# The second half's convolution of chunks 1 to 3 as four TensorE products in a Mamba and mixture-of-experts kernel

## The reference

```python
xn = _layernorm(x)
# s = Mamba block of xn
xr = xn * rsqrt(mean(xn * xn) + eps) * norm_w
xi, z = split(xr @ W_in)                        # 128 -> 256 and 256
xc = silu(causal_conv(xi, conv_w, 4 taps) + conv_b)
dt, Bm, Cm = split(xc @ W_x, [64, 80])          # 64, 16, 16
dt = softplus(dt @ W_dt + b_dt)                 # 256
dA = exp(dt[..., None] * A); dBu = (dt * xc)[..., None] * Bm[:, :, None, :]
h = scan(h = dA * h + dBu)                      # 256 x 16 states, over 256 tokens
y = (einsum('blds,bls->bld', h, Cm) + D_skip * xc) * silu(z)
s = xn + y @ W_out
# g = silu(mixture of experts of xn)
logits = xn @ Wg; top 2 of softmax, normalised -> scores
g = silu(sum_e scores_e * (relu(xn @ W1_e + b1_e) @ W2_e + b2_e))
out = x + s * g
```

## Time and profile before

| | |
|---|---|
| median of 3 runs | 275.86 us (275.59 to 277.68) |
| the profiled execution's own time | 278.05 us |
| its span, first to last instruction | 276.0 us |
| mean granted TensorE clock | 0.968 |
| busy: PE, DVE, ACT, POOL | 252.0, 249.0, 228.3, 237.0 us |
| instructions | 4179 |

### The profile page before, as it was taken

The page is one execution under the profiler, slowest core; times in us unless marked ns, Lnnn a source line. Parts: engine busy times, 40 slices in busy tenths (PEclk is TensorE's granted clock), DMA queues, the critical chain, the costliest instruction groups (busy, mean ns, idle before and its releaser), DMA issues. The chain is left out here.

```text
span 276.0 us, 4179 instructions
## 1 busy us (share of the span) xinstructions
PE 252.0 (91%) x1227; PEld 133.2 (48%) x1227; DVE 249.0 (90%) x284; ACT 228.3 (83%) x436; POOL 237.0 (86%) x191
## 2 busy tenths in 40 slices
PE   7889597699999899899999999789999999999992
PEld 7434241274546433445656426237647446566442
DVE  4696999949799999999999999998799999999994
ACT  1589996989979999999789899996788986878560
POOL 5509699739899999879999999977989997999995
PEclk9999999689999999999999999957999999999999
DMA  5987980024490660024670058070399700000002
GB/s 155 234 250 186 224 203 4 7 77 91 93 207 14 148 159 0 2 70 96 134 180 1 0 126 181 2 161 11 80 207 210 191 2 0 2 0 0 2 1 76
DMA packets 18979, 26.16 MB, mean 95 GB/s; under 512 B 6615, under 2 KB 12174, under 8 KB 18958
## 3 DMA queue, kind: packets, MB, share of 16 engines
q1 hardware_dynamic: 18066, 24.71, 38.1%
q10 hardware_dynamic: 700, 0.66, 1.0%
q0 software_dynamic: 192, 0.52, 0.9%
HBM read 8.65 MB, written 1.31 MB: 36 GB/s over the span
## 5 line engine op out<-in xcount | busy, mean ns | idle before, releaser
L445 POOL TENSOR_TENSOR hc<-hs,Ct 128x1024 f32<-128x1024 f32 x63 | 149.3, 2382 | 5.7 <-DMA Ct<-bc_rows 2.0
L951 DVE TENSOR_TENSOR_SCAN hs<-dec,pdbu 128x1024 f32<-128x1024 f32 x62 | 139.4, 2273 | 0.0
L638 ACT ACTIVATE dec<-rep,negA 128x512 f32<-128x512 f32 x124 | 85.0, 724 | 0.3 <-DMA rep<-dt_u 0.2
L927 DVE TENSOR_TENSOR pdbu<-rep,px 128x1024 f32<-128x1024 f32 x60 | 70.9, 1218 | 8.2 <-PE px L1174 8.1
L1200 PEld LDWEIGHTS px<-w,hT 128*128 128x128 f32 x512 | 62.5, 197 | 14.0 <-issue 8.9
L1194 PE MATMUL px<-xnT,w 128*128 128x512 f32 x128 | 64.9, 614 | 2.2 <-DVE pdbu L927 1.3
L1200 PE MATMUL px<-w,hT 128*128 128x128 f32 x512 | 65.7, 284 | 0.2 <-DVE pdbu L927 0.2
L578 POOL TENSOR_TENSOR acc<-acc,ysc 128x512 f32<-128x512 f32 x30 | 38.3, 1276 | 14.8 <-ACT ysc L752 14.8
L763 ACT ACTIVATE hT<-px,cols 128x512 f32<-128x512 f32 x64 | 43.4, 693 | 8.0 <-PE px L1194 5.5
L752 ACT ACTIVATE ysc<-px,score 128x128 f32<-128x128 f32 x120 | 34.0, 367 | 16.7 <-PE px L1200 16.6
L1083 PE MATMUL py<-hc,rsel 128*32 128x512 f32 x252 | 36.1, 619 | 1.7 <-POOL hc L445 1.7
(11 more groups left out here) (162 smaller groups left out, 275.9 us busy)
## 6 DMA issues: line engine op xcount, KB each, us to landing
rep<-dt_u SPq DMA_DIRECT2D x116, 128.0 KB, 2.4
Ct<-bc_rows SPq DMA_DIRECT2D x16, 256.0 KB, 5.2
w<-in_L_ffn_W SPq DMA_DIRECT2D x1, 1024.0 KB
...
```

Of the source, the lines that this page charges most:

```text
L445: eng.tensor_tensor(hc[:, n % HC_RING], hs[:, n % HS_RING], Ct[:, k % 2, j:j + 1, :].to_broadcast([P, 2, CH]), ALU.mult).then_inc(hc_last ...
L638: act.activation(dec[:, n % DEC_RING, i, :], rep[:, q, 0, :], ACT.Exp, scale=negA[:, q, j:j + 1])\
L927: dve.tensor_tensor(pdbu[:, at:at + 2, :], rep[:, 2 * pair:2 * pair + 2, 1, :], B[:, None, :].to_broadcast([P, 2, CH]), ALU.mult).then_inc ...
L951: dve.tensor_tensor_scan(states.rearrange("p b t -> p (b t)"), dec[:, n % DEC_RING].rearrange("p b t -> p (b t)"), pdbu[:, at:at + 2, :].r ...
```

## The change

`xc1` of chunks 1 to 3 becomes four products like `xc0`, evacuated once by ACT; the tiles `xi`, `add_tap`, the steps `taps` and ACT's wait on `convolved` go. `v0` and `v1` read all 128 rows of `dtp` with a `wdt` that is zero in its lower half (a memset on DVE), and the second copy `dt_low` goes. The selectors of `e0`, `e1` and `spread_u` have 32 rows, at partitions 0 to 31 for the first and 32 to 63 for the second, and both spreads of u follow `e1`; `B1` moves behind them. ACT's queue loads the taps' row second; the rows of three small vectors are issued by POOL; on SP the four `A_log` loads go ahead of the bulk of x. All tables are new.

```diff
-PRE_JOBS = ["tr", "xc0", "xc1", "dt", "v0", "v1", "B0", "B1", "tn", "e0", "e1"]
+PRE_JOBS = ["tr", "xc0", "xc1", "dt", "v0", "v1", "B0", "tn", "e0", "e1", "B1"]
...
-    0: ["gl", "m1b", "m0a", "z0", "z1"], 2: ["m0b", "m1a"], 9: ["gs"], 10: ["gb"],
+    0: ["gl", "m0b", "m1b"], 1: ["z1", "z0", "m1a"], 2: ["m0a"], 10: ["gs"], 13: ["gb"],
...
-    "second": [2], "gate": [1, 2, 2, 2, 2, 3, 5, 5, 6, 6, 9, 9, 9], "gate_e": [0], "gate_p": [8], "third": [10],
+    "second": [3], "gate": [0, 1, 1, 1, 3, 4, 5, 5, 6, 7, 10, 11, 11], "gate_e": [0], "gate_p": [7], "third": [8],
...
-            for b in range(DB):
-                sp.dma_start(wdt[RANK * b:RANK * (b + 1), :], W_dt[:, b * P:(b + 1) * P]).then_inc(w_proj, 16)
-            sp.dma_start(x_sb[:, 1:CHUNKS], xv_dram[:, TPC:TILES, :].rearrange("p (c t) d -> p c t d", t=TPC))\
-                .then_inc(x_in[2], 16)
+            sp.dma_start(wdt[0:RANK, :], W_dt[:, :]).then_inc(w_proj, 16)
             for i in range(GROUP):
                 sp.dma_start(alog[GD * i:GD * (i + 1)].rearrange("p q j s -> p q (j s)"),
                              A_log.rearrange("(q d) s -> d q s", d=GD)).then_inc(w_alog, 16)
+            sp.dma_start(x_sb[:, 1:CHUNKS], xv_dram[:, TPC:TILES, :].rearrange("p (c t) d -> p c t d", t=TPC))\
+                .then_inc(x_in[2], 16)
...
+            pool.dma_start(rows[V_CB:V_CB + 2, :], conv_b.rearrange("(b p) -> b p", p=P)).then_inc(w_rows_soft, 16)
+            pool.dma_start(rows[V_BDT:V_BDT + 2, :], b_dt.rearrange("(b p) -> b p", p=P)).then_inc(w_rows_soft, 16)
+            pool.dma_start(rows[V_DS:V_DS + 2, :], D_skip.rearrange("(b p) -> b p", p=P)).then_inc(w_rows_soft, 16)
...
-                pool.tensor_tensor(sums[:, :, t:], sums[:, :, t:], tap(t).rearrange("p (b t) -> p b t", b=BPC)[:, :, 0:SEQ - t],
-                                   ALU.add).then_inc(convolved, 1)
...
-                        act.activation(xv[:, b, :], src[:, :], ACT.Identity, scale=cw[:, b, TAPS - 1:TAPS],
-                                       bias=cols[:, V_CB + b:V_CB + b + 1]).then_inc(tap_done, 1)
-                        for t in range(1, TAPS):
-                            ins = act.activation(tap(t), src[:, :], ACT.Copy, scale=cw[:, b, TAPS - 1 - t:TAPS - t])
...
-                    ins = act.activation(dt_low[:, :], src[0:RANK, :], ACT.Copy)
+                    ins = act.activation(dtp[0:RANK + 2 * STATES, :], src[0:RANK + 2 * STATES, :], ACT.Copy)
...
-                pe.matmul(pdbu[:, 2 + i, :], copies(i), dt_u[:, 0, 1, :], start=True, stop=True).then_inc(u_spread, 1)
+                pe.matmul(pdbu[:, 2 + i, :], copies(i), dt_u[GD * i:GD * (i + 1), 0, 1, :], start=True, stop=True)\
+                    .then_inc(u_spread, 1)
...
-                elif job == "xc1" and k > 0:
-                    wait_emptied(pe, "tr", k)
-                    last = pe.matmul(dst[:, :], win[:, P:2 * P], xrT[:, :, PAD:PAD + SEQ], start=True, stop=True)
...
-                    last = pe.matmul(dst[:, :], wdt[RANK * b:RANK * (b + 1), :], (dtp[0:RANK], dt_low)[b],
-                                     start=True, stop=True)
+                    last = pe.matmul(dst[:, :], wdt[:, b * P:(b + 1) * P], dtp[:, :], start=True, stop=True)
```

More of the change, by code:

```diff
@@ L69 @@
 }]
 STEPS = [{
-    "silu": [10], "times_dt": [17, 28], "scale_rows": [0], "normalise": [8],
-    "gate": [19, 19, 21, 21, 22, 23, 25, 25, 25, 26, 26, 29, 30], "gate_e": [16], "gate_p": [27],
-    "gate_y": [22, 38], "far": [18, 28], "third": [16], "taps": [7, 7, 10],
-}, {
-    "silu": [11], "times_dt": [15, 25], "scale_rows": [0], "normalise": [2],
-    "gate": [19, 20, 23, 23, 24, 24, 25, 25, 26, 29, 29, 30, 30], "gate_e": [16], "gate_p": [36], "finish": [31],
-    "gate_y": [21, 38], "far": [20, 33], "third": [17], "taps": [3, 4, 8],
-}, {
-    "silu": [11], "times_dt": [17, 21], "scale_rows": [0], "normalise": [5],
-    "gate": [20, 21, 24, 25, 26, 26, 27, 27, 27, 31, 31, 31, 33], "gate_e": [18], "gate_p": [30], "finish": [11],
-    "gate_y": [22, 37], "far": [20, 22], "third": [17], "taps": [1, 7, 8],
+    "silu": [10], "times_dt": [16, 25], "scale_rows": [1], "normalise": [4],
@@ new lines @@
+    "gate": [18, 18, 20, 21, 21, 21, 21, 21, 22, 22, 22, 23, 27], "gate_e": [15], "gate_p": [28],
+    "gate_y": [22, 37], "far": [18, 26], "third": [18],
+}, {
+    "silu": [10], "times_dt": [17, 25], "scale_rows": [0], "normalise": [5],
+    "gate": [20, 20, 21, 22, 23, 23, 24, 24, 24, 25, 26, 27, 29], "gate_e": [17], "gate_p": [29], "finish": [37],
+    "gate_y": [22, 39], "far": [20, 26], "third": [18],
+}, {
+    "silu": [10], "times_dt": [16, 23], "scale_rows": [0], "normalise": [1],
+    "gate": [20, 21, 24, 25, 26, 26, 27, 27, 29, 31, 32, 32, 32], "gate_e": [21], "gate_p": [29], "finish": [12],
+    "gate_y": [22, 38], "far": [16, 23], "third": [16],
@@ L175, in mamba_moe @@
         wtap = sb("wtap", [P, TAPS, DIN])
-        cw = sb("cw", [P, DB, TAPS])
+        cw = sb("cw", [P, TAPS])
         wx = sb("wx", [P, DB, RANK + 2 * STATES])
-        wdt = sb("wdt", [DB * RANK, P])
+        wdt = sb("wdt", [P, DIN])
         wout = sb("wout", [P, DB, D])
@@ L182, in mamba_moe @@
         w2 = sb("w2", [P, EXPERTS, HB, D])
-        b2_all = sb("b2_all", [P, TPC, D])
-        b2d = b2_all[0:TPC * EXPERTS]
-        dt_low = b2_all[P - RANK:P, :, :].rearrange("p t d -> p (t d)")
+        b2d = sb("b2d", [TPC * EXPERTS, TPC, D])
+        rows = sb("rows", [V_END, P])
         cols = sb("cols", [P, V_END])
@@ L221, in mamba_moe @@
         ysc = sb("ysc", [P, YSC_RING, CH])
-        rows = ysc[0:V_END, 0, 0:P]
         csel = ysc[:, YSC_RING - 1, 0:2 * P].rearrange("p (q i d) -> p q i d", q=2, i=GROUP)
@@ L592, in _ @@
                     times_C(pool, n // 2)
-                for k, i in steps_at(n, "taps"):
-                    add_tap(k, i + 1)
                 for k, b in steps_at(n, "times_dt"):
@@ L1178, in fill @@
                     pe.wait_ge(far_done, 1)
-                    last = pe.matmul(dst[:, :], copies(int(job[1])), dt_u[:, 0, 0, :], start=True, stop=True)
+                    q = int(job[1])
+                    last = pe.matmul(dst[:, :], copies(q), dt_u[GD * q:GD * (q + 1), 0, 0, :], start=True, stop=True)
                 elif job == "gs":
@@ L1226, in _ @@
                 keep_busy(BUSY.get(job, 0))
-                if job in ("e0", "e1"):
-                    spread_u(int(job[1]))
+                if job == "e1":
+                    spread_u(0)
+                    spread_u(1)
             for n in range(END_SLOT + 1):
```

46 lines of the change are left out of this document (14 added, 32 removed), and 29 rows, old and new, of the table TABLE.

## The result

The changed kernel takes 286.84 us (median of 3 runs, 286.02 to 287.26) against 275.86: the ratio is 1.039, with an interval of 1.034 to 1.044. The prediction, 275.4 us in a range of 270.5 to 281, was wrong. The profiled execution took 287.26 us with a span of 285.2 us, where the one before had 276.0, at nearly the same mean clock (0.966, before 0.968).

What follows compares the result with a forecast made beforehand. No single engine bounds the kernel: DVE's chain and PE run side by side with hardly any room. Terms +0.6 - 2.9 + 3.9 - 0.5 + 1.8 - 3.1 = -0.2, or -0.6 with cheaper spreads; forecast 275.4 us, range 270.5 to 281.

Steps and rivals of the forecast that it cites:

- The start, +0.6: Up to times_B of units 2 and 3: new order +1.8 us, earlier loads -1.2 us, together +0.6 us.
- The cheaper spreads: Spreads of u on 32 rows may overlap on PE; first scan 0 to 0.8 us earlier, then lost again.
- the vectors' rows: Start: three rows issued by POOL land at about 7.1, needed at 7.11; nothing lost, at worst 1.5 us.
- rows at 5.7: Start: by the Trainium skill's 2.0 us fixed per GpSimd DMA, the vectors' rows land at 5.7, with ample cover.
- dt_u behind the scan: Start: after times_B and the scan to 33.0, dt_u ends at 33.7; times_B of units 2 and 3 follows at 33.8.
- Slot 16, -2.9: First boundary, units 8 and 9: the 4.04 us hole closes, DVE at 56.0 instead of 58.88, -2.9 us.
- Slot 18, +3.9: Between B tiles 4 and 5: gl ends at 65.0, gmx waits 4.4 us, slot 20 at 67.6 instead of 66.64, +3.9 us.
- rival (b): Clock falls ahead of chunk 1's dt (+1.4 us) and near chunk 3's gl (-3.1 not gained): 280 us, chance 0.15.
- Slots 20 to 64: Waits go up to slot 24, -0.5 us; then to slot 64 tight B tiles 10 and 15 to 16, +1.8 us.
- Slot 88, -3.1: Second hole: full clock through gl of chunk 3, three waits of 3.83 us go, 0.7 us comes: -3.1 us.
- (d): Rival at the start: vectors come late from POOL, +1 to 1.5 us, 276.5 us; chance counted within the forecast's 0.47.
- (c): Rival: PE's added work comes out in full, every added product delaying the next tile; 279 to 286, say 281 us; chance 0.13.

Runs made afterwards that it cites:

- E1: Changed kernel with the three loads of the vectors' rows back on ACT's queue, behind the taps' row; 284.79 us, 1.033.
- E10: Kernel before with the changed kernel's whole START line (gate, late u of half 1, gate_p, third), all else as before; 283.41 us, 1.029.
- E9: Changed kernel with only chunk 0's gate steps back at the slots of the kernel before, u of half 1 still late; 280.34 us, 1.016.
- E12: Changed kernel with only the last steps of chunk 0's gate (four grest steps) back at slots 6 and 9; 286.59 us, 1.043.
- E8: Changed kernel with only dt_u (u of half 1) back at slot 2, ahead of the scan of unit 1; 284.96 us, 1.035.
- E3: Changed kernel with the old order of the start: chunk 0's gate steps and u of half 1 back at their old slots; 278.62 us, 1.0095.
- E6: E5 with chunk 1's gate one slot later, so gmx stands behind both scans of units 8 and 9; 279.16 us, 1.014.
- E15: E5 with PE's order changed between slots 14 and 20: v and gl ahead of y1 and m2, B tile 5 one slot earlier; 278.7 us, 1.010.
- E5: Changed kernel with both the old order of the start and the vectors' rows issued by ACT; 278.14 us, 1.010.
- E14: E5 with chunk 0's tables of the kernel before, new tables in chunks 1 to 3; 1.011, median of twelve runs 280.74 us.
- E4: Kernel before with its own tables, start and loads; only xc1 of chunks 1 to 3 is four products, evacuated once; 281.53 us, 1.020.
- E13: Kernel before with the new tables, xc1 still one product with GpSimd sums, xc1 and xc0 exchanged in chunk 1; 284.01 us, 1.030.

## Why the prediction was wrong, point by point

**The start, +0.6: the step that failed.** It measured +6.7 us at slot 4. The order was read rightly, and the hole before gvs came as forecast (2.35 us, forecast 2.4). The cheaper spreads took 2.4 us (23.11 to 25.50 on PE) instead of 3.6, not half. Three things were missing. First, the vectors' rows: "nothing lost, at worst 1.5 us" was 2.12 us of PE's wait, and with the clock that fell behind it 3.3 us at times_B of unit 1 against E1 (28.72, where the forecast's terms give 29.6 - 1.2 = 28.4), and 1.6 us of the whole time. The other forecast there, rows at 5.7, was 2.4 to 4 us too early: they were used at 8.05 to 9.66. The bound took 3.7 us for the landing, from another DMA of this queue; it measured 4.5 to 6.2. Second, dt_u behind the scan was costed at 0.7 us. The row for times_B at 31.96 showed 4.51 us for two, where 2.36 is usual; it was used as a position and never as a question. It is the collision with POOL, and in the new order DVE meets POOL's products twice, with dt_u and with times_B of unit 2, and they take 4.0 us more than usual instead of 2.2. Third, nothing was booked for what a late start does behind it, on POOL and PE. The scan of unit 2 came late, POOL's product waited 4.70 us for it and PE's reduce 4.16 us for POOL, the clock fell, and B tile 3 was 1.82 us late where the prediction had 0.3. Nor does the hole at slot 16 absorb such a delay: in E10 it grows from 4.04 to 6.82 us, partly through the gate's last steps, because PE's work for tile 4 hangs on the same POOL and DVE steps.

Of the 8.1 us that the order costs, 6.4 go with the gate's order (E9), of which the tail is worth nothing (E12), and the rest with the late u (E8). It was a mechanism that none of the rivals had.

**Slot 16, -2.9.** The hole closed, no wait at 63.18. Slots 4 to 16 took 24.6 us (E3: 23.1), forecast 23.4; the 1.2 us above it are about the lateness of B tile 3.

**Slot 18, +3.9.** The wait for gl is there, with 6.55 us for the forecast's 4.4; slots 16 to 20 took 5.9 us more than before. The term was under-sized by 2 us. y0 and y1 took 5.18 us instead of 3.9, with the clock at 0.56 behind PE's pauses of 2.35 and 1.46 us for ACT, and those pauses themselves were not in the sum, as ACT's silus and two table loads stand ahead of sT. This is rival (b)'s first place, priced there at 1.4. E6 and E15 show that the position of gmx and gl is not what binds; PE's stretch from dt to B tile 6 is, its work at the clock that it gets there.

**Slots 20 to 64.** -0.7 and +1.3 measured, -0.5 and +1.8 forecast. Right.

**Slot 88, -3.1.** -0.9 in the changed kernel, -2.5 in E3. The clock did hold through gl of chunk 3, as forecast (gl took 1.06 us at 194.59, before 1.88 at 184.67), but behind gl it was low from 196 to 202, which is 186 to 192 in the old times, so a wait of 1.87 us stayed; with the start repaired it was 0.40. Sized rightly for the repaired kernel only.

**Chunk 3, 0.** -0.6. Right.

**The sum.** It also had a slip: the positions 56.0 and 67.6 already held the 0.6 us of the start, which was then added again. By the stretches it was -0.8, not -0.2. That is small beside the rest.

**The rivals.** (d), late vectors, happened, at more than its price. (b) happened at its first place, and in part at the second. (c), PE's work in full, has the price nearest to the measured time, but the runs show another cause for most of it. (c) may be what is left: with the start repaired the kernel stays 1% (2.8 us) over the one before in five variants (E3, E5, E6, E14, E15), whose order differs and whose work doesn't. That PE's added work is its cause is supported by E4 and E15 and not isolated, since E13 fails to give the time back. Nor is the clock isolated: E3, with a low clock from 56 to 60, has slot 24 at 77.53, and E5, with one from 52 to 62, at 79.03. This stays open.
